# One block from the second gated stage to the end of the kernel: the softmax's first unit inside the norms, its last batch inside the third gated stage

## What is computed

```
x = x + 0.5 * L0_ffn(norm(x))    # 32 small experts, top 4 by sigmoid gate
x = x +       L0_attn(norm(x))   # linear attention, 16 heads
x = x + 0.5 * L0_ffn(norm(x))
x = x + 0.5 * L1_ffn(norm(x))    # 8 experts of 512, top 2, capacity limit
x = x +       L1_attn(norm(x))   # below
x = x + 0.5 * L1_ffn(norm(x))
```

```
logits = einsum('bhmk,bhnk->bhmn', Q, K) * sqrt(64)      # causal
key_weights = softmax(logits, axis=-1)
o = einsum('bhmm,bhmv->bhmv', key_weights, V)             # the token's own weight times its own V
y = einsum('bhmv,hdv->bmd', o, P_o)
```

## Time and profile before

| | us |
|---|---|
| median of 3 runs | 1787.54 |
| lowest and highest run | 1783.36, 1790.53 |
| the profiled execution, whole | 1795.37 |
| its span, first to last instruction | 1793.6 |
| first half (before f1) | 0 to about 440 |
| f1 | about 440 to 700 |
| first experts, first combine | about 700 to 893, to 938 |
| softmax | 938 to about 1421 |
| a1o | about 1422 to 1576 |
| second experts, last combine | 1576 to 1767, to 1793.6 |

### The profile page before, as it was taken

How to read it: one execution, slowest core, us unless ns; L and a number is a source line. 1 busy time by engine, 2 the same in 40 slices (tenths; PEclk the granted TensorE clock), 3 DMA queues, 4 the chain that set the end, 5 groups by cost and what they waited for, 6 DMA issues and landing times. The chain is left out here.

```text
span 1793.6 us, 30589 instructions
## 1 busy us (share of the span) xinstructions
PE 1441.7 (80%) x8651; PEld 1048.8 (58%) x8653; DVE 1343.0 (75%) x3826; ACT 1077.9 (60%) x2260; POOL 858.8 (48%) x742
## 2 busy tenths in 40 slices
PE   5899988896999994998527888888888699679880
PEld 4677767654666653776415666566566466357660
DVE  7588887565667666776676999999999667757766
ACT  6677752364122325777437999999999522267770
POOL 6666642210034343565626666666666124636663
PEclk9899998898999996999859999999999899789995
DMA  5997001000001114222129930000000001122225
GB/s 106 142 176 115 1 1 25 1 1 24 16 30 43 30 33 93 55 67 60 41 85 183 179 59 1 1 1 1 1 1 1 1 16 34 42 59 59 59 57 143
DMA packets 182175, 91.71 MB, mean 51 GB/s; under 512 B 43829, under 2 KB 176902, under 8 KB 182048
## 3 DMA queue, kind: packets, MB, share of 16 engines
q1 hardware_dynamic: 167840, 71.19, 21.5%
q0 software_dynamic: 9984, 16.89, 2.9%
q10 hardware_dynamic: 4224, 2.10, 0.4%
HBM read 32.59 MB, written 61.18 MB: 52 GB/s over the span
## 5 line engine op out<-in xcount | busy, mean ns | idle before, releaser
L2523 DVE CUSTOM_DVE_ANT_0 psum<-psum,cmask 128x128 f32<-128x128 f32 (+7 forms) x512 | 375.5, 786 | 28.5 <-PE psum L2433 28.1
L2494 ACT ACTIVATE psum<-psum,gate 128x128 f32<-128x128 f32 (+7 forms) x512 | 367.0, 719 | 41.2 <-DVE gate L2523 33.8
L2180 POOL DMA_INDIRECT answers<-ed,answer_to x184 | 198.0, 1076 | 71.7 <-issue 45.4
L1258 PE MATMUL psum<-raw_all,w 128*128 128x512 f32 x384 | 195.4, 592 | 3.1 <-DVE raw_all L1383 1.5
L628 PE MATMUL psum<-xl,wreg 128*128 128x512 f32 x320 | 182.8, 571 | 11.2 <-PEq L89 10.9
L1173 POOL TENSOR_TENSOR hl<-hg,hh 128x512 fp32r<-128x512 f32 x96 | 124.4, 1296 | 83.1 <-ACT hh L1089 80.3
L1381 DVE SCALAR_TENSOR_TENSOR raw_all<-psum,hg 128x512 f32<-128x512 f32 x128 | 88.1, 691 | 70.3 <-PE psum L630 67.2
L174 POOL TENSOR_TENSOR spare_p<-spare_p 128x1 f32<-128x1 f32 x62 | 21.3, 344 | 226.3 <-DVE row_no L750 109.4
L629 PE MATMUL psum<-xh,wreg 128*128 128x512 f32 x320 | 127.3, 398 | 0.0
L630 PE MATMUL psum<-xh,wreg 128*128 128x512 f32 x320 | 127.0, 397 | 0.0
L2433 PE MATMUL psum<-spare_sets_room 64*128 64x384 f32 (+3 forms) x768 | 93.1, 375 | 41.9 <-ACT psum L2494 41.9
(11 more groups left out here) (410 smaller groups left out, 4046.1 us busy)
## 6 DMA issues: line engine op xcount, KB each, us to landing
rows<-blank SPq DMA_DIRECT2D x146, 258.0 KB, 7.1
row<-rows SPq DMA_DIRECT2D x46, 256.0 KB
raw_all<-answers SPq DMA_DIRECT2D x32, 256.0 KB, 3.4
w<-in_L_ffn_W_dram SPq DMA_DIRECT2D x16, 256.0 KB
answers<-ed,answer_to POOLq DMA_INDIRECT x184
x<-in_L_attn_x_dram SPq DMA_DIRECT2D x4, 512.0 KB, 5.7
out_dram<-x ACTq DMA_DIRECT2D x8, 256.0 KB
rawD<-in_L_ffn_values_dram SPq DMA_DIRECT2D x4, 256.0 KB, 7.0
```

The lines of the kernel that those rows point to most:

```text
L1258: pe.matmul(bank(B_OUT[i % 2]), col(dn, j), hidden[:, n % HID, :], start=(j == 0), stop=(j == nf - 1)).then_inc(S["dn_done"], 1)
L2180: pool.indirect_dma_start(answers, bass.IndirectOffsetOnAxis(ap=answer_to[:, out.odd, t:t + 1], axis=0), y_row[:, out.odd, t, :], None, bo ...
L2494: return act.activation(src, src, ACT.Exp, bias=kept_at(arg, u, q, a), scale=-1.0, accum_out=kept_at(esum, u, q, a))
L2523: return dve.tensor_tensor_reduce(src, src, mask, 1.0, 3e38, ALU.add, ALU.min, kept_at(arg, u, q, a))
```

## The change

The three last phases become one block, `second_half`. Each engine goes through all its stages in order, without a clear or a barrier between them. So that semaphore numbers suffice, the two experts' stages share theirs (but `y_sent`), and GpSimd clears 26 of them in the middle of the softmax. What moves, besides:

- The norms behind the first experts: a root on ScalarE and one correction step in place of the twelve steps; even blocks are normalised on VectorE and odd ones on ScalarE, into `later` (which holds all blocks), and turned in banks 4 to 7. After block 3 each engine does its part of the softmax's first unit (`opening`): the projections and the copies out.
- The softmax: batches 0 to 2 are finished (reciprocal, exponent, product, copy) inside the units of the following batch. The last batch is finished inside the first block of a1o (`closing`), whose first gates wait only for batch 0.
- The experts: `leave` stands one place earlier. `heads_low` moves into the opening iteration, behind a new GpSimd operation that follows the last send. The first block's weights are copied at the start of that iteration. Fewer of the last blocks have paced sends.
- f1: `moe_low` of the next expert goes before `send_rows`, and `MOE_AT` is 7 for 10.

```diff
-    MOE_AT = 10
+    MOE_AT = 7
...
+                else:
+                    pe.wait_ge(ahead["p_kept"], i // (NB // BATCH) + 1)
                 spread_gates(pe, bank(B_G), i).then_inc(S["g_done"], 1)
 
...
+                    if i == 0 and closing:
+                        closing.tensor(pe, j)
                     if i == 0 and j == 2:
...
             dve.tensor_tensor(L, L, kept_rs[:].unsqueeze(2).to_broadcast([P, NT, E1]), ALU.mult).then_inc(S["logits_scaled"], 1)
-            if first:
-                heads_low(dve, H)
             positions(dve, S)
...
+            if first:
+                moe_low(pool, M, 0)
+            else:
+                pool.wait_ge(ahead["blanked"], 16 * (ROWS // BLK))
             for k in range(NB):
-                if first:
-                    moe_low(pool, M, k)
+                if first and k + 1 < E1:
+                    moe_low(pool, M, k + 1)
                 send_rows(pool, k, S, paced)
+            if first:
+                pool.wait_ge(S["spaced"], NB)
+                apart(pool, spare_p).then_inc(S["spaced"], 1)
...
                     dve.value_load(expert_of[0:1, bass.ds(k.n + 1, 1)], min_val=0, max_val=E1 - 1) if k.there() else None
                     for k in (last, b, nxt))
+                opening = not b.loop and b.c == -1
+                if opening:
+                    up_weights(nxt, e_next, 0)
+                    up_weights(nxt, e_next, 1)
+                    if before["heads"]:
+                        dve.wait_ge(before["spaced"], NB + 1)
+                        heads_low(dve, before["heads"])
                 for j in range(Q):
                     if j == 0 and last.there():
                         low(last, Q - 1)
                     if j >= 1 and b.there():
                         low(b, j - 1)
+                    if j == 1 and out.there():
+                        leave(out)
                     if j == 0 and nxt.there():
                         next_low(nxt)
                     for k in range(2):
-                        if j == UP_AT[k] and nxt.there():
+                        if j == UP_AT[k] and nxt.there() and not opening:
                             up_weights(nxt, e_next, k)
                         if j == DOWN_AT[k] and b.there():
                             down_weights(b, e_now, k)
-                    if j == LEAVE_AT and out.there():
-                        leave(out)
                     if j == 3 and last.there():
                         answer_bias(last, e_last)
 
...
                     for t in range(BT):
-                        if t and out.n + 2 <= SPARSE:
+                        if t and out.n + 4 <= SPARSE:
...
+            act.activation(var[:], mv[:, :, 1], ACT.Sqrt, bias=ln_eps[:])
...
+                for t in range(BT):
+                    at = i * BT + t
+                    last = act.activation(normal[:, at, :], x[:, at, :], ACT.Identity, bias=v_all[:, at:at + 1],
+                                          scale=y_all[:, at:at + 1])
+                last.then_inc(S["xn_act"], 1)
+
+            def high(i):
+                act.wait_ge(S["xT_done"], i + 1)
+                act.activation(xh[:, blk(i)], bank(B_XT[i % 4]), ACT.Copy).then_inc(S["xh_done"], 1)
+
+            act.wait_ge(S["gathered"], 1)
+            act.activation(z_all, aggr[:, :, 1], ACT.Sqrt, bias=ln_eps[:]).then_inc(S["root"], 1)
+            act.wait_ge(S["shifted"], 1)
+            normalise(1)
             for i in range(NB):
-                split_act(act, S, i)
+                high(i)
+                if i % 2 and i + 2 < NB:
+                    normalise(i + 2)
+                if i == 3:
+                    beside.scalar(act)
 
         def vector(dve):
             n = 0
...
-            then(gather(dve, NB - 1, S["measured"]))
-            deviations(dve, then)
-            split_dve(dve, S)
+            gather(dve, NB - 1, S["measured"]).then_inc(S["gathered"], 1)
+            dve.wait_ge(S["gathered"], 1)
+            then(dve.tensor_scalar(v_all, aggr[:, :, 1], LN_EPS, None, ALU.add))
+            dve.wait_ge(S["root"], 1)
+            then(dve.reciprocal(y_all, z_all))
+            then(dve.tensor_tensor(z_all, y_all, y_all, ALU.mult))
+            then(dve.scalar_tensor_tensor(z_all, z_all, -0.5, v_all, ALU.mult, ALU.mult))
+            then(dve.scalar_tensor_tensor(y_all, z_all, 1.5, y_all, ALU.add, ALU.mult))
+            dve.scalar_tensor_tensor(v_all, aggr[:, :, 0], -1.0, y_all, ALU.mult, ALU.mult).then_inc(S["shifted"], 1)
+
...
+                for t in range(BT):
+                    at = i * BT + t
+                    last = dve.tensor_scalar(normal[:, at, :], x[:, at, :], aggr[:, at, 0:1], y_all[:, at:at + 1],
+                                             ALU.subtract, ALU.mult)
+                last.then_inc(S["xn_dve"], 1)
+
+            def low(i):
+                dve.wait_ge(S["xh_done"], i + 1)
+                dve.tensor_tensor(xl[:, blk(i)], bank(B_XT[i % 4]), xh[:, blk(i)].bitcast(F32), ALU.subtract
+                                  ).then_inc(S["xl_done"], 1)
+
+            normalise(0)
+            normalise(2)
+            for i in range(NB):
+                low(i)
+                if i % 2 and i + 3 < NB:
+                    normalise(i + 3)
+                if i == 3:
+                    beside.vector(dve)
...
-            if not final:
-                split_pe(pe, S)
+            for i in range(0 if final else NB):
+                pe.wait_ge(S["xn_act" if i % 2 else "xn_dve"], i // 2 + 1)
+                wait_past(pe, S["xl_done"], i - 3)
+                for t in range(BT):
+                    last = pe.transpose(tiles(B_XT[i % 4])[:, t, :], normal[:, i * BT + t, :], ident[:])
+                last.then_inc(S["xT_done"], 1)
+                if i == 3:
+                    beside.tensor(pe)
...
+            split(0)
+            for u in range(1, UNITS):
+                split(u)
+                if u == UNITS // 2:
+                    pool.wait_ge(S["blanked"], 16 * (ROWS // BLK))
+                    for one in used:
+                        pool.sem_clear(one)
...
+            if k == 0 and v < 2:
+                pe.wait_ge(split["xl_done"], 2 if v == 0 else NB)
...
+            pe.wait_ge(S["exp_done"], UNITS * NS - 2)
...
+        def exp_own(act, b):
+            act.wait_ge(S["arg_set"], b + 1)
+            act.activation(batch_of(arg, b), batch_of(arg, b), ACT.Exp).then_inc(S["all_exp"], 1)
+
+        def invert(dve, b):
+            dve.wait_ge(S["exp_done"], (b + 1) * PAIRS * NS)
+            dve.reciprocal(batch_of(esum, b), batch_of(esum, b)).then_inc(S["inverted"], 1)
+
+        def divide(dve, b):
+            dve.wait_ge(S["inverted"], b + 1)
+            dve.wait_ge(S["all_exp"], b + 1)
+            dve.tensor_tensor(batch_of(arg, b), batch_of(arg, b), batch_of(esum, b), ALU.mult).then_inc(S["p_set"], 1)
+
+        def keep(dve, b):
+            dve.wait_ge(S["p_set"], b + 1)
+            dve.tensor_copy(batch_of(esum, b), batch_of(arg, b)).then_inc(S["p_kept"], 1)
+
+        def arguments(dve, b, src):
+            all_t = batch_of(arg, b).rearrange("p (c k) e -> p c k e", k=2)
+            dve.wait_ge(S["exp_done"], (b + 1) * PAIRS * NS)
+            dve.tensor_tensor(all_t, all_t, turned_own(src), ALU.subtract).then_inc(S["arg_set"], 1)
+
+        B_OWN = 6
+
+        def end_pe(pe, j):
+            if j == 0:
+                pe.wait_ge(S["exp_done"], UNITS * NS)
+                turn_own(pe, PER - 1, bank(B_OWN)).then_inc(S["own_turned"], 1)
+
+        def end_act(act, j):
+            if j == 3:
+                exp_own(act, PER - 1)
+
+        def end_dve(dve, j):
+            if j == 1:
+                invert(dve, PER - 1)
+            if j == 2:
+                dve.wait_ge(S["own_turned"], 1)
+                arguments(dve, PER - 1, bank(B_OWN)[:, 0:2 * P])
+            if j == 5:
+                divide(dve, PER - 1)
+            if j == 6:
+                keep(dve, PER - 1)
+
...
+                    copy_out_act(act, u + 1)
+                for n, q in enumerate(ORDER):
+                    if n == 2 and u > 0 and u % PAIRS == 0:
+                        exp_own(act, u // PAIRS - 1)
...
+                    copy_out_dve(dve, u + 1)
+                for n, q in enumerate(ORDER):
+                    done = u // PAIRS - 1
+                    if done >= 0 and n == 1 and u % PAIRS == 0:
+                        invert(dve, done)
+                    if done >= 0 and n == 1 and u % PAIRS == 1:
+                        divide(dve, done)
+                    if done >= 0 and n == 3 and u % PAIRS == 1:
+                        keep(dve, done)
                     for a in range(2):
...
+    def second_half():
+
+        names = ("scaled", "summed", "added", "step", "measured", "gathered", "root", "shifted", "xn_act", "xn_dve", "xT_done", "xh_done",
+                 "xl_done")
+        split = {n: sem("m0c_" + n) for n in names}
```

(13 more changed lines are left out.)

389 lines of the change are left out of this document (198 added, 191 removed).

## The result

The changed kernel takes **1755.76 us** (median of 4 runs, 1753.99 to 1757.95) where the kernel before takes 1786.49 on the same chip: ratio 0.983, 95% interval 0.980 to 0.985, so 30.7 us less. I had forecast 1768 us and 1757 to 1779; the direction was right, the gain 1.6 times as large. The profiled execution of after took 1756.6 us, its span is 1754.8 us: 38.8 us less than that of before. That difference is larger than that of the medians, since the profiled execution of before, 1795.37 us, lies above all its timed runs.

A forecast was written before the change was run, and what follows sets the result against it. The softmax was taken as bound by a TensorE-VectorE-ScalarE ring, other stretches by no full engine, so edges should gain: -1.5 - 1.4 - 1.0 - 11 + 2.5 - 7 = -19.4 us off 1787.54, 1768 us, range 1757 to 1779.

The forecast's parts named there:

- Part 1: Before the first experts: moving heads_low shortens a long GpSimd send, -1.5 us (0 to -1.6); earlier moe_low gives nothing.
- The zero by which the send had another cause: Last sends before the experts: by the skill's rule two-input operations do not stall descriptor generation, so the gain would be 0.
- Part 2: Experts' blocks: earlier leave gains only at the stages' ends, -1.4 us and -1.0 us; 0 per block in the loop.
- Rival (d): Experts' blocks: earlier leave frees turned bank and rows' buffer, 0.25 us for each of 46 blocks, 1757 us; chance 0.09.
- Part 3: Norms and first softmax unit: shorter norms and earlier unit 0 bring the first minimum sooner, -11 us (-8 to -12.2).
- a second chain through unit 1's projections: Norms to softmax: turns 4 to 7, low parts, then unit 1's projections put unit 0's scores at 940 or 942.3 us.
- the clock term: Unit 0's projections, four groups, taken at the low clock: 5.25 us, from 926.3 to 931.4.
- Part 4: Inside the softmax ring: finishing batches 0 to 2 there adds 3 x 0.83 = +2.5 us (+0.75 to +5).
- rival (b): Softmax ring passes on more than the added steps' time: +8 for +2.5, 1773.5 us; chance 0.07.
- rival (c): The port: leave before two casts puts a block's first send beside them, gains at the sends lost, 1772 us; chance 0.06.
- Part 5: Softmax to third gated stage: gates wait only for batch 0, closing steps stand between products, -7 us (-6 to -8).
- Rival (e): Experts' 46 blocks: a wait in leave holds low part and weight copies, 0.65 us a block, 1798 us; chance 0.03.

The follow-up runs named there:

- kind B: Chips on which the kernel before takes about 1762 us; there the kernel after, unchanged, took 1743.83 us, ratio 0.989.
- kind A: Chips on which the kernel before takes 1786 to 1791 us, among them the chip of the first runs.
- b_to: Kernel before, leave in its old place, with an index buffer for each block so SyncE no longer waits for GpSimd's sends: 1779.77 us, ratio 0.996.

## Why the prediction was right in sign and too small

- **Part 1** (-1.5, measured -4.5 in this pair of traces, -3.5 in the pair of kind B, -3.0 between the means of all). The long send went as forecast: from the first to the last send -1.5 to -1.9 us in all traces. The zero by which the send had another cause is out. A step that failed is "`moe_low` one period earlier [...] uses the same gap between the sends of two blocks as now: nothing". I asked only what GpSimd had free, not what VectorE did beside it: 3.0 us at that place, with 1.3 to 3.1 lost again earlier in the stage in the two traces that can be compared.
- **Part 2** (-2.4, measured -13 to -19 on kind A, -3.1 on kind B). This is the step that made the forecast fail: "In the loop GpSimd has time to spare and nothing follows: 0 per block". Something follows: SyncE's index load waits for the sends, and the row load stands behind it; that wait taken away by itself gave 7.3 us (b_to), so it carries a part and the rest stays open. SyncE's wait of 149.0 us was in the profile and I did not use it. Rival (d) came nearest, with 1757 us from 0.25 us a block, where 13 to 19 us over 46 blocks are 0.28 to 0.41; but it named the turned bank and the rows' buffer, and what came free sooner was the index buffer, ahead of the row load in SyncE's queue. That its number fits is luck of the chip: on kind B it would have been 0.07 a block. How much it is depends on late steps, SyncE's above all, that vary between chips; one profile could not tell that, but its block periods of 5.9 to 10.9 us could have warned me. At the last blocks themselves the gain is small: GpSimd's run of sends behind the last weight copies starts 0.4 us sooner against them than before (1.8 us behind, at 1711.85, for 2.1), not 1.4, since the block before still held it.
- **Part 3** (-11, measured -13.5 here, -12.1 to -13.5 in the twelve traces). The chain was right, with GpSimd's split last; in before as in after the first minimum starts 1.3 us behind its end, and that alone gives my lower end, 941.6, or 23.2 us behind the statistics. I took 942.8, for a second chain through unit 1's projections that decided in none of the traces: 1.2 us. The other 1.3 are the clock term: unit 0's projections took 2.8 us, not 5.25, since the clock happened to rise before them in this execution and three others.
- **Part 4** (+2.5, measured +6.5 in the mean). The list of the causes was in the wrong order: I gave the reciprocal 0.45 us a batch and the copy 0.25. The reciprocal was hidden, and the copy cost 1.97. That comes nearest to rival (b) in size, and to rival (c)'s port in mechanism, at a place where I had not looked.
- **Part 5** (-7, measured -6.6 from last exponent to first product, -6.0 in the pair of kind B, with the clock in it). Right in size; the overlap that I named for it is worth about 1 of it.
- Rival (e), that the leave holds the queue behind it, and (c) at the sends did not happen: the 184 sends of answers took 1.09 us in the mean in after and 1.08 in before.
- The errors in parts 1, 3 and 4 (-3.0, -2.5, +4.0) nearly cancel. What took the time below my range, by 1.2 us, is part 2; on kind B, where it is small, the whole gain was 18.2 us, and the 19.4 of my sum would have been right, in part because these errors cancel.

**Open:** why SyncE and at times ScalarE step late on some chips and not on others, and what a send of GpSimd has to do with it. Outside the two expert stages the traces of before on kind A and kind B differ by 0.4 to 2.8 us a stretch, inside by 13 to 14. With written-out blocks most of it is gone, but they also take away register work (432 such instructions of SyncE for 614; mean step 1.40 us on kind A, against 1.59 with loops on kind B), so the 20 us are not all cured stalls. That the loops are the cause is not shown: some late steps are left without them, the earlier leave alone brings the stages to 168 and 169 us with the loops in place, and written-out blocks were not run on kind B. Whether the earlier leave still pays with written-out blocks was not run.
